# Token mixing and routed experts on one core: expert results kept in the tiles' own rows, and the first twos of tiles placed among the attention's last links

## What is computed

```python
h = tok(x, W, b, cls_token, pos_enc); h = concatenate([h, txt], axis=1)
n = layernorm(h)
Q, K, V = elu(n Wq + bq) + 1, elu(n Wk + bk) + 1, n Wv + bv        # 16 heads of 16
h = h + (Q (K^T V) / (Q sum(K) + 1e-6)) Wo + bo
n = layernorm(h)
logits = n @ gate_w.T; sel = argmax(logits); rw = sigmoid(max(logits))
xs = n * rw                                                       # for the expert sel
h = h + (xs @ w_up[sel].T * silu(xs @ w_gate[sel].T)) @ w_down[sel].T
```

## Time and profile before

| | us |
|---|---|
| median of 3 runs | 491.35 (490.98 to 492.08) |
| the profiled execution | 497.19 |
| its span, first to last instruction | 495.4 |
| TensorE busy | 447.8 (90%) |
| VectorE busy | 379.2 (77%) |
| ScalarE busy | 259.9 (52%) |
| GpSimd busy | 290.3 (59%) |

### The profile page before, as it was taken

How to read it: one execution, slowest core, us unless ns; L and a number is a source line. 1 busy time by engine, 2 the same in 40 slices (tenths; PEclk the granted TensorE clock), 3 DMA queues, 4 the chain that set the end, 5 groups by cost and what they waited for, 6 DMA issues and landing times.

```text
span 495.4 us, 12152 instructions
## 1 busy us (share of the span) xinstructions
PE 447.8 (90%) x3728; PEld 438.1 (88%) x3728; DVE 379.2 (77%) x1208; ACT 259.9 (52%) x642; POOL 290.3 (59%) x662
## 2 busy tenths in 40 slices
PE   4999999999999999999999999999679898887650
PEld 4999999999999999999999999999679888887540
DVE  5649579889988989989999988977686766556440
ACT  5344446556667766766746656665354443335100
POOL 6305224766776776776776776664564555554563
PEclk9999999999999999999999999999899998999955
DMA  8962121424231231121121121076134752111110
GB/s 286 289 211 82 56 57 58 121 70 122 63 100 47 72 93 33 34 61 39 33 61 39 37 61 46 21 194 195 40 124 147 215 187 84 67 67 58 65 67 23
DMA packets 35006, 46.13 MB, mean 93 GB/s; under 512 B 8937, under 2 KB 27100, under 8 KB 34944
## 3 DMA queue, kind: packets, MB, share of 16 engines
q1 hardware_dynamic: 25722, 30.23, 20.5%
q0 software_dynamic: 9216, 15.12, 9.9%
q10 hardware_dynamic: 6, 0.01, 0.0%
HBM read 26.61 MB, written 17.17 MB: 88 GB/s over the span
## 4 chain that ended last, share of the span: by engine, by line
PE 76%; DVE 6%; issue 6%; another core or an unknown queue 3%; POOL 3%; DMA 2%; ACT 1%; POOLq 0%; SPq 0%; DVEq 0%; ACTq 0%
PE b_w L1372 7%; PE b_w L1370 7%; PE b_att L1420 7%; PE b_w L1371 6%; PE b_kg L1370 6%; PE b_kg L1372 6%; PE b_kg L1371 6%; PE b_att L1484 5%; PE b_v L1372 3%; PE b_v L1370 3%; PE b_v L1371 3%; PE b_t L1433 2%; PE b_t L1498 2%; PE b_att L1370 2%
## 5 line engine op out<-in xcount | busy, mean ns | idle before, releaser
L720 POOL DMA_INDIRECT out<-result,rows_all x64 | 62.3, 973 | 52.4 <-DVE result L1279 31.7
L655 POOL DMA_INDIRECT sorted_rows<-rows,place x64 | 75.3, 1176 | 20.5 <-POOL place L652 10.6
L908 ACT ACTIVATE silu_g<-b_kg,rows_all 128x128 f32<-128x128 f32 x64 | 20.2, 370 | 49.6 <-PE b_kg L1372 29.8
L828 ACT ACTIVATE q_exp<-b_w,bq_s 128x228 f32<-128x228 f32 x64 | 28.9, 451 | 31.7 <-PE b_w L1372 31.7
L1370 PE MATMUL b_kg<-wkgv_hi,xnT_hi 128*114 128x264 f32 x128 | 41.9, 327 | 0.0
L616 POOL TENSOR_SCALAR ve<-mv 114x2 f32<-114x2 f32 x32 | 7.3, 228 | 58.1 <-DVE mv L1001 58.0
L1370 PE MATMUL b_w<-wo_hi,attnT_hi 128*114 128x264 f32 x124 | 41.0, 330 | 0.0
L1370 PE MATMUL b_kg<-wgu_hi,xsT_hi 128*128 x128 | 37.1, 290 | 3.2 <-DVE act_u L1289 2.2
L1370 PE MATMUL b_w<-xnT_hi,wq_hi 128*128 128x256 f32 x128 | 38.7, 302 | 1.4 <-DVE logits L1079 1.1
L1370 PE MATMUL b_v<-wkgv_hi,xnT_hi 128*114 128x256 f32 x128 | 38.8, 303 | 0.0
L811 ACT ACTIVATE den<-b_att,z_eps 114x32 f32<-114x32 f32 x32 | 9.2, 287 | 55.4 <-PE b_att L1484 52.9
(11 more groups left out here) (243 smaller groups left out, 1759.7 us busy)
## 6 DMA issues: line engine op xcount, KB each, us to landing
rows_all<-sorted_rows SPq DMA_DIRECT2D x64, 130.0 KB
rows_all<-in_x SPq DMA_DIRECT2D x18, 384.0 KB, 4.1
rows_all<-in_txt SPq DMA_DIRECT2D x32, 154.0 KB
rows_all<-in_wgu SPq DMA_DIRECT2D x8, 256.0 KB, 2.8
rows_all<-patch_out SPq DMA_DIRECT2D x48, 36.0 KB
sorted_rows<-tail_rows SPq DMA_DIRECT2D x9, 130.0 KB
rows_all<-in_wdown SPq DMA_DIRECT2D x8, 128.0 KB, 3.2
sorted_rows<-rows,place POOLq DMA_INDIRECT x64
```

What stands on the lines that cost most here:

```text
L655: G.indirect_dma_start(out=scratch[0:EXPERTS * REGION, :], out_offset=bass.IndirectOffsetOnAxis(ap=place[:, k, b:b + 1], axis=0), in_=rows ...
L720: G.indirect_dma_start(out=out, out_offset=bass.IndirectOffsetOnAxis(ap=rows_all[:, t.n, ID:ID + 1].bitcast(I32), axis=0), in_=result[:, k ...
L828: S.activation(q_exp[:, c, :], at, ACT.Exp, bias=bq_s[:, c:c + 1])
L908: last = S.activation(silu_g[:, t.slot(4)], b_gu[m.slot(2)][:, t.slot(2) * D:t.slot(2) * D + INNER], ACT.Silu, scale=rows_all[:, t.n, GAIN ...
```

## The change

The ring `result` is dropped. The result of a tile is written over the tile's own 256 values in `rows_all`, and the store reads it from there; the wait for `stored` goes. On TensorE `load_experts` stands behind the gate and up products of its step instead of ahead. Steps -3 to 3 of every engine but GpSimd are placed earlier among the last links of the attention; the written-out rest begins at step 4 (GpSimd's steps 2 and 3 are empty).

```diff
-            result = sb("result", [P, 4, D], at=room)
-        STEPS_B = range(2, DUOS + 5)
+        STEPS_B = range(4, DUOS + 5)
...
-                            in_=result[:, k, :], in_offset=None,
+                            in_=rows_all[:, t.n, 0:D], in_offset=None,
...
             attention_high(PAIRS - 2)
             S.activation(silu_ahead[:], bq_s[:, 0:1], ACT.Silu)
+            duo_step(Turn(0, -3))
             tanh(PAIRS - 4)
             denominators(PAIRS - 1)
+            duo_step(Turn(0, -2))
             centred(PAIRS - 3)
             tanh(PAIRS - 3)
             attention_high(PAIRS - 1)
-            straight(range(-3, 1), duo_step)
+            straight(range(-1, 1), duo_step)
             centred(PAIRS - 2)
             tanh(PAIRS - 2)
-            duo_step(Turn(0, 1))
+            straight(range(1, 3), duo_step)
             centred(PAIRS - 1)
             tanh(PAIRS - 1)
+            duo_step(Turn(0, 3))
             straight(STEPS_B, duo_step)
...
                     dve.wait_ge(down_done, m.upto())
-                    if m.had(2):
-                        for t in tiles_of(m):
-                            dve.wait_ge(stored[t.slot(4)], 16 * t.rounds(4, 4))
                     for t in tiles_of(m):
                         at = t.slot(2) * D
-                        last = V.scalar_tensor_tensor(result[:, t.slot(4)], rows_all[:, t.n, 0:D], rows_all[:, t.n, MEAN:MEAN + 1],
+                        last = V.scalar_tensor_tensor(rows_all[:, t.n, 0:D], rows_all[:, t.n, 0:D], rows_all[:, t.n, MEAN:MEAN + 1],
...
             places(PAIRS - 4)
             attention_low(PAIRS - 2)
             queries(PAIRS - 1)
+            duo_step(Turn(0, -3))
             route(PAIRS - 3)
             attention(PAIRS - 1)
             residual(PAIRS - 2)
             gate_logits(PAIRS - 2)
+            duo_step(Turn(0, -2))
             places(PAIRS - 3)
             route(PAIRS - 2)
             attention_low(PAIRS - 1)
+            duo_step(Turn(0, -1))
             stats_2(PAIRS - 2)
-            duo_step(Turn(0, -3))
+            duo_step(Turn(0, 0))
             residual(PAIRS - 1)
             gate_logits(PAIRS - 1)
             places(PAIRS - 2)
             route(PAIRS - 1)
-            straight(range(-2, 0), duo_step)
+            duo_step(Turn(0, 1))
             places(PAIRS - 1)
             late_count()
             stats_2(PAIRS - 1)
-            duo_step(Turn(0, 0))
+            duo_step(Turn(0, 2))
             late_slots()
-            duo_step(Turn(0, 1))
+            duo_step(Turn(0, 3))
             late_rows()
             straight(STEPS_B, duo_step)
...
             def duo_step(j):
-                g = DUO * j.n // EXPERT_LOAD + 1
-                if j.slot(EXPERT_LOAD // DUO) == 4 and 1 < g < TILES // EXPERT_LOAD:
-                    load_experts(g)
                 if j.within(DUOS):
...
                     last.then_inc(gu_done, 1)
+                g = DUO * j.n // EXPERT_LOAD + 1
+                if j.slot(EXPERT_LOAD // DUO) == 4 and 1 < g < TILES // EXPERT_LOAD:
+                    load_experts(g)
...
             turn_attention(PAIRS - 2)
+            duo_step(Turn(0, -3))
             apply(PAIRS - 1)
             project_out(PAIRS - 2)
             load_experts(1)
+            duo_step(Turn(0, -2))
             rank(PAIRS - 3)
             turn_attention(PAIRS - 1)
-            duo_step(Turn(0, -3))
+            straight(range(-1, 1), duo_step)
             rank(PAIRS - 2)
             project_out(PAIRS - 1)
-            straight(range(-2, 0), duo_step)
+            duo_step(Turn(0, 1))
             rank(PAIRS - 1)
             late_count()
-            duo_step(Turn(0, 0))
+            duo_step(Turn(0, 2))
             late_slots()
-            duo_step(Turn(0, 1))
+            duo_step(Turn(0, 3))
             straight(STEPS_B, duo_step)
```

## The result

The changed kernel took 499.62 us (498.13 to 500.50, 4 runs) beside 491.72 us for the kernel before (490.98 to 495.38, 4 runs). The ratio is 1.0127, 95% interval 1.0080 to 1.0174: slower by a little over 1%, and clear of the noise. (The two medians alone would give 1.0161.

What follows compares the result with a forecast made beforehand. TensorE's own rate was taken as the floor, with the kernel up to 1.07 us a two above it from waits and stalls; +1.8 - 0.9 - 3.1 - 0.7 = -2.9 us gave 488.4 us, range 484.8 to 495.3 us.

Steps and rivals of the forecast that it cites:

- early twos: Steps -3 to 3 among the attention's last links: longer chain uses up TensorE's head start, +1.8 us (0 to +3.9).
- registers: `load_experts` of groups 2 and 3 moved behind the gate and up matmuls, hidden there: -0.9 us (0 to -1.8).
- ring, with the end: Dropping the wait on `stored` brings TensorE's 3.1 us; the last twelve stores going back to back bring 0.7 us.
- The four gaps: TensorE's waits on `b_w` before the end, 0.94, 0.24, 1.42 and 0.54 us, 3.14 us together, booked as gain.
- The lower bound of that step: Pessimistic bound for dropping the wait on `stored`: +2.9 us, eight tile pairs by 0.36 us in the stretch to 410 us.
- rival 1: Stalls without a releaser set the pace and the ring only spaces them: +1.1 us, 492.4 us, chance 0.30.
- Rival 1's worst: The stretch to 410 us partly takes on the later stretch's slower pace, 2.9 us: 495.3 us; no separate chance given.
- The signs named for rival 1: Longer "remote" waits of ScalarE and about the same matmuls per us from 384 to 470 us; no size given.
- a two: One `Turn` of the expert pipeline, two tiles; 24 TensorE matmuls and transposes, 2.83 us right after the start.
- the low clock: TensorE idle 2 to 3 us before the gate matmuls of two 5, then half clock for 3.4 us: loses 1.7 us.
- 0.88 us piece: TensorE idle ending with `gu` of two 12; hidden by moving the first `load_experts` behind 12 matmuls: -0.9 us.
- The end: Last twelve stores, 14.81 us, would go back to back in 14.08 us with GpSimd the bound: -0.7 us.

Runs made afterwards that it cites:

- the ring alone: Kernel before with results written over the tiles' rows and no wait for landed stores, old order and `load_experts` place: 498.03 us, ratio 1.0106 (chip 12).
- the three with the wait on the same chip: New order alone 492.67 us (1.0013), `load_experts` moved alone 492.90 us (1.0011), changed kernel with wait put back 495.42 us (1.0023); ratios against the kernel before.
- the paced one: Results in place without VectorE's wait, GpSimd issuing a store only when the one three before landed: 473.99 us, 0.9871 (chip 8); 494.92 us, 1.0037 (chip 14).

## Why the prediction was wrong

By parts, each ratio alone times 492.80 us:

| part | forecast, us | measured, us |
|---|---|---|
| early twos | +1.8 | +0.6 (-1.0 to +2.3) |
| registers | -0.9 | +0.5 (-1.1 to +2.2) |
| ring, with the end | -3.8 | +5.2 (+2.8 to +7.6) |
| sum | -2.9 | +6.4 |
| the change itself, first result | | +6.3 (+3.9 to +8.6) |

**The ring: the step that failed.** It was the sentence "What goes is the wait on `stored`. It brings TensorE's 3.1 us." The four gaps were read as a cost that falls away with its cause. They were real, and they did go: the ring alone has no such wait that ends before 473 us. But in the eight early twos its trace has 30.32 us beside 25.18 to 26.35 us in the three with the wait on the same chip. That the wait earned this by holding GpSimd's stores apart fits the groups of four and six above; it is argued from them, and the wait's effect itself is what is shown. The lower bound of that step, rival 1's, had this mechanism. It had its place as well, the stretch to 410 us taking on the pace of the later one. Its size was short: I gave it eight twos by 0.36 us, 2.9 us. By the turns, the eight twos of that stretch took 3.21 us each in the trace of before and 3.81 us after, 4.8 us together, which is even more than the 3.68 us of the later fifteen in the trace of before. So "in part" should have been "wholly". Rival 1's worst, 495.3 us, was the top of my range, and the measured ratio puts even the low end of its interval, 1.0080 x 491.35 = 495.3 us, right at it.

The signs named for rival 1 came: from 384 to 470 us 548 matmul records beside 559 before, and ScalarE's waits on "remote" 36.2 us in all beside 27.6 us.

One argument for the rival was a misreading, though, and that it came out on the right side is luck. The forecast has a two at 3.28 us "where VectorE's ring waits are longest" and at 3.90 us elsewhere. By their places in the trace the ring's waits were 4.3 us from 384 to 410 us and 7.8 us from 410 to 470 us, about 0.5 us a two in both, and 7.7 us after 470 us; the longest before 470 us, 2.66 us, is in the later stretch. So the two stretches don't compare a kernel with and without the wait. What the rows did hold is that the kernel stood far above TensorE's own rate with no engine full. I took the waits at their face value, since VectorE's and TensorE's stood side by side. That they stand side by side says only that the one passes to the other. It doesn't say that nothing waits behind.

**The early twos: order right, the low clock in another place.** The forecast said what would hold the new order up, and the changed kernel shows each step, in order of time:

```profile
348.21 0.46 PE L1486 MATMUL b_att<-kv_sb,qT 128*114 128x136 f32 x2 [1.44 <-issue]
...
359.00 0.17 DVE L1126 TENSOR_TENSOR chosen<-ranked,first 114x16 bf16<-114x16 f32 x1
...
365.21 0.25 DVE L1003 BATCH_NORM_AGGREGATE mv<-stats 114x2 f32<-114x6 f32 x2
...
370.93 0.20 POOL L630 TENSOR_TENSOR top_n<-top,ratio 114x2 f32<-114x2 f32 x1
...
371.16 0.20 ACT L767 ACTIVATE tanh_top<-top_n 114x2 f32<-114x2 f32 x1 [4.13 <-POOL top_n L630]
...
372.83 0.38 PE L1372 MATMUL b_kg<-wgu_hi,xsT_hi 128*128 x1 [1.48 <-DVE act_u L1288]
```

- The piece ahead of `apply(31)` was to shrink from 1.88 to about 1.45 us with the clock staying up: 1.44 us, and 1.00 from 350.4 to 360.9 us, where the earlier trace rows has 0.86.
- T, the end of `chosen` of pair 31, is 359.17 us. The attention ran 1.37 us ahead in this execution (the cast `attnT_hi` of pair 30 starts at 346.36 us, in the trace of before at 347.73 us); so the forecast's 360.75 us would be 359.38 us here, and what can be compared further on are the differences to T.
- `mv` ends at 365.46 us, T + 6.3; forecast T + 6.3.
- `tanh(31)` starts at 371.16 us, T + 12.0; forecast T + 12.15.
- The gate matmuls of two 5 start at 372.83 us, T + 13.66; forecast T + 13.8. The late loads begin at 378.02 us, and no row turn waits for them.

What failed is the place of the low clock. TensorE's idle before two 5 was 1.48 us and not 2 to 3 us, and from 371.5 to 380 us the clock is 1.00. The long idle piece stands earlier, 2.37 us ahead of the matmuls of `late_slots`, and there the clock did fall. The order of time, then two more stretches of the changed kernel:

```profile
364.45 0.20 PE L1684 MATMUL b_att<-con_s,tiles_f 8*1 8x17 f32 x2 [2.37 <-DVE tiles_f L1313]
```

```profile
364.45:368.00 3.55, 3.55 (x19) 3.46 (x20) 3.45 (x12) 0.91 (x2) 2.21 (x9) 0.53 0.46 148
368.00:371.50 3.50, 3.35 (x29) 3.14 (x27) 0.21 (x1) 0.34 (x2) 2.61 (x4) 0.99 0.59 174
```

At 0.53 for 3.55 us TensorE loses 1.7 us, just the amount forecast. But it is lost ahead of two 5, which waits for VectorE and GpSimd in any case; the slow matmuls fill part of TensorE's wait, of which 1.48 us are left. By that reading the low clock costs nothing. The time can't confirm it: the order alone measured +0.6 us, and its interval, -1.0 to +2.3 us, has both nothing and the forecast's +1.8 us in it. The forecast had no row of TensorE between `rank(31)` and two 5 and so put the idle at the end of the chain.

**Registers.** The 0.88 us piece of the earlier trace rows was to be gained. It is gone in the changed kernel and with `load_experts` moved alone (the gate matmuls of two 12 start at 396.62 us there, with no idle before them). The time of the latter measured +0.1%, +0.5 us with an interval from -1.1 to +2.2 us, which doesn't exclude the forecast's -0.9 us. If nothing was gained, the gap may have been handed on to the next stall; that isn't shown.

**The end.** The last twelve stores were to be back to back, 14.08 us. They take from 472.40 to 488.34 us, 15.94 us, with two waits of 1.1 and 1.4 us for a result in between, where the earlier trace rows has 14.81 us. Two results come late, so GpSimd isn't yet the bound there.

**What stays open.** Stalls are in the traces on four of the five chips tried (11, 12, 13, 14). The runs tie them to the stores by leaving these out (chip 11) or thinning them (chip 13), and exclude the bytes (chip 14). They don't show whether it is the closeness of the stores or their number in a given time, what in the chip makes ScalarE and TensorE stop, nor why chip 8 doesn't. Nor do they show why the ring's wait helps only in the twos to about 409 us; the late loads run there, and no run leaves these out. The changed kernel itself wasn't run on chip 8; three kernels there that also lack the ring's wait were 1.3% to 2.2% faster than before, though two of them store less or fix the weights, and only the one with three stores under way computes all of it (0.9871). That the change gains on such a chip is likely from that, and not shown. No kernel was clearly better than both on all chips: the paced one is 1.3% faster on chip 8 and 1.0037 (0.9993 to 1.0081) on chip 14.

## What to carry to other kernels

A wait that paces an engine may be worth more than it costs. Before a gap is booked as a gain, ask what is behind it: here the kernel stood 17.0 us above TensorE's floor over 23 twos, and the gaps to be gained were 3.1 us of that. Waits on "remote", or on "issue" in the middle of one product, are a sign that something outside the order of the semaphores sets the pace; then test it by leaving the suspected traffic out, which took one kernel here, ahead of pricing any gap. Measure by a stretch with a fixed amount of work, as the eight and the 23 twos here: it told kernels apart whose times overlapped. And place each wait in time before calling a stretch free of it. And run the kernel on more than one chip: a 2.7% difference between chips was larger than the 1.0% to 1.9% that this change moves.

## What the hardware showed unexpectedly

- Stops of ScalarE and TensorE without a releaser come with GpSimd's indirect stores, issued every 1.28 us in a group: on the four chips that show them, 23 twos took from 77 to 86 us in the traces with all stores, 67.61 us with three quarters of them (chip 13), and 63.80 us with half (chip 13) or none (chip 11).
- The number of bytes made no difference: with a quarter of them the 23 twos took 85.54 us, with all of them 85.36 us on the same chip.
- From 384 to 410 us TensorE's granted clock was 1.00 in all four traces with the ring's wait and 0.93 in all six of the changed kernel and the ring alone; in the changed kernel it fell right behind stops of 1.14 and 1.05 us close together.
- On one chip of five (8), none of the four kernels profiled has them; the kernel before, which wasn't profiled there, took 479.36 us on it and 489.84 to 492.80 us on the others.
- TensorE kept its full clock over idle pieces of 1.44 and 1.48 us in the changed kernel, as over 1.70 us before; after 2.37 us it ran at 0.53, as at 0.54 after 1.88 us before. The low clock at 364.45 us stood ahead of a wait of TensorE that still lasted 1.48 us.
